# Attention scores of four heads at once in float32, in place of split operands stacked by DMA

## What is computed

```
def _L2_gnn_ref(X, A, Wp, bp, C):          # 8 heads, 32 features each
    Xp = jnp.einsum('bnd,hdk->bhnk', X, Wp) + bp[None, :, None, :]
    Xc = jnp.einsum('bhnk,hjk->bhnj', Xp, C)
    attn = jnp.tanh(A[:, None] * jnp.einsum('bhnj,bhmj->bhnm', Xc, Xp))
    Xh = jnp.einsum('bhnm,bhmk->bhnk', attn, Xp)
    out = jnp.moveaxis(Xh, 1, 2).reshape(X.shape[0], X.shape[1], -1)
    return jax.nn.relu(out)
```

## Time and profile before

| | us |
|---|---|
| median of 3 runs | 1858.39 (1857.15 to 1858.89) |
| span of the profiled execution | 1856.2 |
| PE busy | 1539.5 (83%) |
| DVE busy | 1339.2 (72%) |
| ACT busy | 787.7 (42%) |
| POOL busy | 274.1 (15%) |
| mean granted TensorE clock | 0.924 of full |

### The profile page before, as it was taken

One profiled execution on the slowest core, in us unless ns is written; L12 is line 12 of the kernel. 1 busy time (PEld: TensorE's weight loads), 2 busy tenths in 40 slices (PEclk: granted clock), 3 DMA queues, 4 the chain that ended last, 5 costly groups with the idle time before them and its releaser, 6 DMA issues.

```text
span 1856.2 us, 27152 instructions
## 1 busy us (share of the span) xinstructions
PE 1539.5 (83%) x9334; PEld 1185.5 (64%) x9334; DVE 1339.2 (72%) x3050; ACT 787.7 (42%) x1271; POOL 274.1 (15%) x167
## 2 busy tenths in 40 slices
PE   4587988979798898988989898897989789798855
PEld 3486665757667575766757676675767667576632
DVE  5666868777686877768687776868767686876623
ACT  2224436353453635335353533535353363534432
POOL 1101120111202011120201112020111201012010
PEclk9788999989899898989989898998989899898977
DMA  5013131132313203231320323123031312313030
GB/s 158 12 52 80 52 100 65 38 78 73 90 51 97 67 34 79 73 90 51 86 78 34 79 73 90 51 73 91 23 90 63 101 51 61 83 43 80 22 81 11
DMA packets 80806, 125.52 MB, mean 68 GB/s; under 512 B 10176, under 2 KB 29184, under 8 KB 80768
## 3 DMA queue, kind: packets, MB, share of 16 engines
q1 hardware_dynamic: 80768, 125.02, 24.0%
HBM read 66.27 MB, written 8.39 MB: 40 GB/s over the span
## 4 chain that ended last, share of the span: by engine, by line
PE 56%; DVE 16%; issue 13%; ACT 6%; POOL 5%; SPq 2%; DMA 1%; DVEq 0%; POOLq 0%; ACTq 0%
PE ring_f L1023 32%; PE ring_b L1023 16%; DVE att L969 6%; PE pv_acc L1289 2%; PE ring_f L1179 1%; POOL xp_s L445 1%; POOL xf L428 1%; POOL xf L426 1%; PE ring_f L1209 1%; DVE rows L898 1%; ACT att L596 1%; DVE rows L879 1%; PE ring_f L1121 1%; ACT uz L472 1%; DVE hf L850 1%
## 5 line engine op out<-in xcount | busy, mean ns | idle before, releaser
L1023 PE MATMUL ring_f<-m,inc_n 128*128 128x256 f32 x2048 | 324.2, 288 | 17.0 <-POOL m L418 14.4
L969 DVE TENSOR_TENSOR att<-ring_b,at 128x1024 f32<-128x1024 f32 x256 | 299.2, 1216 | 31.1 <-PE ring_b L1023 30.5
L575 ACT ACTIVATE att<-att 128x1024 f32<-128x1024 f32 x256 | 263.7, 1066 | 100.3 <-DVE att L969 94.4
L1023 PEld LDWEIGHTS ring_f<-m,inc_n 128*128 128x128 f32 x2048 | 289.2, 194 | 25.4 <-issue 21.0
L1023 PE MATMUL ring_b<-stk_c,stk_p 96*128 96x512 f32 x512 | 183.7, 477 | 61.1 <-DMA stk_c<-xc_s 44.5
L1023 PE MATMUL ring_f<-m,inc_t 128*128 128x256 f32 x1024 | 210.3, 284 | 14.5 <-DVE m L728 14.5
L1023 PE MATMUL ring_f<-w,uz 128*128 128x256 f32 (+1 forms) x896 | 188.1, 333 | 13.0 <-DVE uz L721 8.4
L1023 PEld LDWEIGHTS ring_b<-stk_c,stk_p 96*128 96x128 f32 x512 | 97.7, 217 | 147.3 <-issue 70.1
L407 POOL TENSOR_TENSOR rstd_f<-var_f,mhalf 128x4 f32<-128x4 f32 x48 | 48.5, 1010 | 933.2 <-DVE var_f L715 933.2
L1023 PEld LDWEIGHTS ring_f<-w,uz 128*128 128x128 f32 x896 | 151.6, 191 | 34.0 <-DVE uz L721 14.8
L1023 PEld LDWEIGHTS ring_f<-m,inc_t 128*128 128x128 f32 x1024 | 160.4, 191 | 17.7 <-DVE m L728 17.7
(11 more groups left out here) (163 smaller groups left out, 2656.7 us busy)
## 6 DMA issues: line engine op xcount, KB each, us to landing
stk_p<-xp_s SPq DMA_DIRECT2D x192, 128.0 KB, 2.4
stk_c<-xc_s SPq DMA_DIRECT2D x192, 128.0 KB, 2.3
rows<-in_adjT SPq DMA_DIRECT2D x16, 1024.0 KB, 5.3
adj_n<-in_adj SPq DMA_DIRECT2D x16, 1024.0 KB, 8.5
at<-in_adjT SPq DMA_DIRECT2D x16, 1024.0 KB, 5.2
x_in<-in_x SPq DMA_DIRECT2D x16, 512.0 KB, 3.5
out_x<-xb SPq DMA_DIRECT2D x16, 512.0 KB, 2.9
wrow<-in_adj SPq DMA_DIRECT2D x16, 256.0 KB, 6.0
```

Source lines behind the costliest of these rows:

```text
L575: act.activation(v, v, ACT.Tanh).then_inc(tanh_made.sem, 1)
L969: dve.tensor_tensor(att[:, u % 2, 2 * half:2 * half + 2], pair(tile)[:], at[:, t].unsqueeze(1).broadcast_to([P, 2, N]), ALU.mult)\
L1023: ins = pe.matmul(dst, lhsT, rhs, start=(first and n == 0), stop=(last and n == len(pairs) - 1), skip_group_check=True)
```

## The change

The scores are computed in float32 from xp and xc as they are, without split and without stacking. A head's 32 features lie on 32 partitions of its own, so the four heads of a tile use four different groups of 32 array rows, and write four different PSUM banks. Gone are the 24 DMAs of a graph with their two semaphores, the high part of xp on DVE, its low part on POOL and the low part of xc on DVE. ACT writes xp to a buffer of its own (xp_t), and xc with one copy to xc_t. k_scores now waits for both pairs of banks before its first product, where it waited for the second pair after the products of the first. The split of the fourth layer, which used stk_c too, goes to ax_s with unchanged instructions.

```
--- before.py
+++ after.py
@@ buffers and counts @@
-        xp_s = sb("xp_s", [P, 2, 2 * N], F32R)
+        xp_t = sb("xp_t", [P, 2, N])
+        xc_t = sb("xc_t", [P, 2, N])
         xc_s = sb("xc_s", [P, 2, 2 * N], F32R)
-        stk_p = sb("stk_p", [P, HEADS, N], F32R)
-        stk_c = sb("stk_c", [P, HEADS, N], F32R)
+        ax_s = sb("ax_s", [P, 4, N], F32R)
...
@@ SyncE @@
-            def stack(dst, src, part, group, loaded):
-
-                for h in range(4):
-                    sp.dma_start(
-                        dst[32 * group:32 * group + 32, h:HEADS:4, :].bitcast(F32),
-                        src[32 * h:32 * h + 32, part, :].rearrange("p (t n) -> p t n", t=2).bitcast(F32),
-                    ).then_inc(loaded.sem, 16)
-
-            def stack_p(g):
...
-                stack(stk_p, xp_s, 0, 0, stk_p_loaded)
-                stack(stk_p, xp_s, 0, 1, stk_p_loaded)
-                sp.wait_ge(xp_lo_made.sem, xp_lo_made.after(g, 1))
-                stack(stk_p, xp_s, 1, 2, stk_p_loaded)
-
-            def stack_c(g):
...
@@ GpSimd @@
-            def k_xp(g):
-                pool.wait_ge(xp_hi_made.sem, xp_hi_made.after(g, 1))
-                pool.tensor_tensor(xp_s[:, 1], att[:, 0, 0:2].rearrange("p t n -> p (t n)"),
-                                   xp_s[:, 0].bitcast(F32), ALU.subtract).then_inc(xp_lo_made.sem, 1)
@@ ScalarE @@
-                    ins = act.activation(att[:, 0, c], pair(B_XP)[:, c], ACT.Identity, bias=bp_c[:, c:c + 1],
+                    ins = act.activation(xp_t[:, c], pair(B_XP)[:, c], ACT.Identity, bias=bp_c[:, c:c + 1],
                                          scale=1.0)
...
-                act.activation(xc_s[:, 0], pair(B_XC)[:].rearrange("p t n -> p (t n)"), ACT.Copy)\
-                   .then_inc(hi_b_made.sem, 1)
+                act.activation(xc_t[:], pair(B_XC)[:], ACT.Copy).then_inc(copied_b.sem, 1)
@@ VectorE @@
-            def k_xp(g):
...
-                dve.tensor_copy(xp_s[:, 0], att[:, 0, 0:2].rearrange("p t n -> p (t n)")).then_inc(xp_hi_made.sem, 1)
-
-            def k_xc(g):
-                dve.wait_ge(hi_b_made.sem, hi_b_made.after(g, 2))
-                dve.tensor_tensor(xc_s[:, 1], pair(B_XC)[:].rearrange("p t n -> p (t n)"), xc_s[:, 0].bitcast(F32),
-                                  ALU.subtract).then_inc(drained_b.sem, 1)
...
@@ TensorE @@
             def k_scores(g, u):
                 part, t = divmod(u, NT)
                 if u == 0:
-                    pe.wait_ge(stk_p_loaded.sem, stk_p_loaded.after(g, STACK_LOADS))
-                    pe.wait_ge(stk_c_loaded.sem, stk_c_loaded.after(g, STACK_LOADS))
-                for half in range(2):
-                    ps = bank_b(g, B_S + 2 * u + half)
-                    for k in range(2):
-                        h = 4 * part + 2 * half + k
-                        ins = products(ps[:, k], [(stk_p[0:STACK, h, t * P:(t + 1) * P], stk_c[0:STACK, h])])
-                    ins.then_inc(full_b.sem, 1)
+                    pe.wait_ge(copied_b.sem, copied_b.after(g, 2))
+                pairs = [bank_b(g, B_S + 2 * u + half) for half in range(2)]
+                for h in range(4):
+                    rows_of = slice(h * KH, (h + 1) * KH)
+                    ins = pe.matmul(pairs[h // 2][:, h % 2], xp_t[rows_of, part, t * P:(t + 1) * P],
+                                    xc_t[rows_of, part], start=True, stop=True, skip_group_check=True)
+                    if h % 2 == 1:
+                        ins.then_inc(full_b.sem, 1)
```

More of the change, by code:

```diff
@@ L191, in back_drained_at @@
         def back_drained_at(tile):
-            return {B_HT: 1, B_XC: 2, B_OT: 19, B_TT: 20}.get(tile, tile - B_S + 3)
-        STACK_LOADS = 3 * 4
-        STACK = 3 * KH
+            return {B_HT: 1, B_OT: 18, B_TT: 19}.get(tile, tile - B_S + 2)
         x_loaded = Signal(sem("x_loaded"), 1, 16)
@@ L589, in k_ax @@
                 act.wait_ge(full_b.sem, full_b.after(g, B_TT + 1))
-                act.activation(stk_c[:, 0:2], pair(B_TT)[:], ACT.Copy).then_inc(hi_b_made.sem, 1)
+                act.activation(ax_s[:, 0:2], pair(B_TT)[:], ACT.Copy).then_inc(hi_b_made.sem, 1)
             def k_out(g):
@@ L959, in k_unit @@
                     dve.wait_ge(at_loaded.sem, at_loaded.after(g, 1))
-                    dve.wait_ge(xp_lo_made.sem, xp_lo_made.after(g, 1))
-                    dve.wait_ge(full_b.sem, full_b.after(g, B_XN + 1))
                 if u == 1 and seen(g, 1):
@@ L995, in k_ax @@
             def k_ax(g):
-                dve.wait_ge(hi_b_made.sem, hi_b_made.after(g, 3))
-                dve.tensor_tensor(stk_c[:, 2:4], pair(B_TT)[:], stk_c[:, 0:2].bitcast(F32), ALU.subtract)\
+                dve.wait_ge(hi_b_made.sem, hi_b_made.after(g, 2))
+                dve.tensor_tensor(ax_s[:, 2:4], pair(B_TT)[:], ax_s[:, 0:2].bitcast(F32), ALU.subtract)\
                    .then_inc(drained_b.sem, 1)
@@ L1061, in bank_b @@
                                B_O: (B_OT, 0)}.get(tile, (tile - 2, 0))
-                if before in (B_XP, B_XN, B_O):
+                copied = {B_XP: 1, B_XC: 2, B_XN: 3, B_O: 4}
+                if before in copied:
                     if seen(g, ago):
-                        pe.wait_ge(copied_b.sem, copied_b.after(g, {B_XP: 1, B_XN: 2, B_O: 3}[before], ago=ago))
+                        pe.wait_ge(copied_b.sem, copied_b.after(g, copied[before], ago=ago))
                 else:
@@ L1267, in k_xc @@
                 for t in range(2):
-                    ins = products(ps[:, t], [(ct[:, t], att[:, 0, t])])
+                    ins = products(ps[:, t], [(ct[:, t], xp_t[:, t])])
                 ins.then_inc(full_b.sem, 1)
@@ L1281, in k_attend @@
                 if u == 0:
-                    pe.wait_ge(copied_b.sem, copied_b.after(g, 2))
+                    pe.wait_ge(copied_b.sem, copied_b.after(g, 3))
                     if seen(g, 1):
@@ L1327, in k_out @@
                         v = slice(i * P, (i + 1) * P)
-                        pairs += three(stk_c[:, c, v], stk_c[:, 2 + c, v], k3[:, 0, c], k3[:, 1, c])
+                        pairs += three(ax_s[:, c, v], ax_s[:, 2 + c, v], k3[:, 0, c], k3[:, 1, c])
                     ins = products(ps[:, i // 2, (i % 2) * D:(i % 2 + 1) * D], pairs)
```

34 lines of the change are left out of this document (8 added, 26 removed).

## The result

| | before | after |
|---|---|---|
| median of the runs, us | 1858.64 (1857.15 to 1859.56) | 1879.86 (1875.58 to 1880.77) |
| span of the profiled execution, us | 1856.2 | 1878.1 |
| mean granted TensorE clock | 0.924 | 0.94 |

The ratio is 1.0109, with a 95% interval of 1.0097 to 1.0121: the change makes the kernel slower by 21 us. Less work is left to do, and yet it takes longer: the DMAs moved 125.5 MB before and move 75.2 MB now, VectorE's busy time fell from 1339.2 to 1314.4 us and PE's from 1539.5 to 1520.5. PE's mean clock is higher, so it waits more.

A forecast was written before the change was run, and what follows sets the result against it. PE, busy 83% of the span, sets a turn by its order of work. Gross +2.2 less 1.3 from the clock, +0.9 times 15 turns (+13.5), and -7 in the last part gave 1865 us; range 1850 to 1890.

The forecast's parts named there:

- rival (C): Full turns: the clock gives nothing back or returns late; 2.2 us a turn, 1884, up to 1900 us; chance 0.14.
- The DMA wait is covered: PE's 2.46 us wait before k_scores 0 is covered by the 2.56 us ReLU wait before f_hT; gain taken as 0.
- (B): Rival: the DMA wait before k_scores 0 was on the path; -2.46 us a turn, 1815 us; chance 0.04.
- The removed vector work is worth nothing: Removed DVE and POOL parts of xp and xc stand in gaps; removing DVE's 1.22 us only lengthens its wait; gain 0.
- A unit's release at 1.22 us: Score units: DVE may begin 1.22 us after a unit's start, as all four heads finish together; bounds 1.14 to 3.4 plus release.
- The walk through the turn, gross +2.2: From f_hT to k_outT, later releases and the wait for both pairs add 2.2 us a turn; bounds 1.8 to 3.3.
- The clock gives back 1.3: Shifted work lets PE's clock return earlier in the program, saving 1.3 us a turn; net +0.9.
- The bound of 1.85: Most the clock could give back in a full turn: 1.14 + 0.7 = 1.85 us.
- The last back part, -7: Last back part, no front work: 14 us gained on the DMA wait, 7 lost on units and lower clock; -7.
- The sum: Whole kernel: 1856.2 + 13.5 - 7 = 1862.7 us span; runs lie 2.2 above it, 1865 us; chance 0.46.
- (D): Rival: score units' row groups do not run at once; 1985 us, or about 2125 fully in turn; chance 0.12.

The follow-up runs named there:

- e3: Kernel before without its 24 stacking DMAs a graph, score products reading 96 rows of the split operands where they lie: 1845.27 us, 0.9923 of before.
- e7: Kernel after, each pair of banks waited for just ahead of its two heads, with 22 and 9 unused products filling PE's gaps: 1843.08 us, 0.9910 of before.
- e10: Kernel before with 10, 12, 9 and 5 unused products filling PE's gaps: 1832.85 us, 0.9857 of before.
- e9: Kernel after with pair-by-pair waits, 22 and 9 unused products, and one small 128-row product between a unit's second and third product: 1889.63 us, 1.0172 of before.
- e5: Kernel after with 22 unused products ahead of f_hT and 9 between k_out and k_xp: 1863.28 us, 1.0016 of before.
- e8: Kernel after with all four heads of a unit reading array rows 0 to 31, one row group: 2368.3 us, 1.2735 of before.
- e4: Kernel after with 22 unused products between k_scores 0 and f_hT only: 1864.63 us, 1.0030 of before.
- e1: Kernel after with each pair of banks waited for just ahead of its own two products, as in the kernel before: 1860.1 us, 1.0004 of before.

## Why the prediction was right or wrong

The time lies in the range, 15 us above the forecast, and that is in part luck: the forecast was a slowdown of 7 us and 21 were measured, three times as much. The range held it because it was wide enough to take in most of rival (C), at 1884, to which the result is nearest. The place of the loss and its gross size were right; what the clock gives back was not.

- **The DMA wait is covered: right.** f_hT stands 11.00 us behind f_y's start as before, and e3 shows full turns that do not change when the DMAs go. (B) is out.
- **The removed vector work is worth nothing: right.** DVE was 25 us less busy, and k_xp to f_hT, where its removed work stood, is as long in e7 as in e10 (31.26 and 31.25).
- **A unit's release at 1.22 us: measured 1.17**, between the bounds. Its cause was wrong, as e9 shows.
- **The walk through the turn, gross +2.2: right,** 2.15 in a late turn and 33.1 / 15 = 2.2 over the run, between e5 and e10. The parts hold too: the forecast let DVE be idle some 1.2 us before units 6 and 7 (measured 1.23 and 1.23) and had ACT late last before k_outT (1.11 us of idle time on PE, ended by xh_t's copy, where it was 0.81). Unit 2 was to be late by 0.60; against k_attend 0, which was 0.90 us earlier after f_hT, DVE's start moved by 0.40.
- **The clock gives back 1.3: this step failed.** It measured 0.4 a turn in the late turns and 0.24 over the run. The step was built on one early turn that was 1.14 us shorter, and on the thought that a longer program keeps drifting past the good place, and stops there. It did stop, but in a pattern of two turns, of which one keeps the stretch to 5.8 us past f_hT. And the 1.14 was read wrongly. The forecast took it as what the stretch behind f_hT gives back, but that turn has 31.05 us (251.68 to 282.73, rows below) from k_xp to f_hT, where a late turn has 31.86, for the clock was at its upper level behind k_xp (1.00 from 251 to 256 us). Only 0.42 us lie behind f_hT (39.83 us to k_outT and not 40.25). The bound of 1.85 was set too high: behind f_hT the clock costs a late turn of before 1.1 us in all, and 1.66 in the whole turn, so 1.3 was more than there was to give behind f_hT. To take it was to expect the whole cost to vanish, with PE idle for longer ahead of f_hT (5.84 us against 2.46 and 2.56).
- **The last back part, -7: measured -8.0** from the last copy of xc_s. The gain was 13.9 for a forecast 14; the units lost 7.4 for a forecast 4.9 plus 2 for the clock; the 1.3 us won behind the units were in no term. The cycle is 3.74 us (1837.20 to 1840.94) and not 3.53, since DVE idles 1.38 and not 1.26.
- **The sum.** 15 turns by 0.9 were 15 by 1.97 (2.2 - 0.24), 29.5 us for 13.5: that is 16 us too few, less 1 for the last part: the 15 by which the time lies above the forecast.
- **(D): refuted** by 1.07 us a unit, and priced by e8. Its upper end, 2125, does not follow from its own terms: 17 a turn by 15, less 7, is 2106.

The two rows of the early turn, k_xp and f_hT, in the kernel before:

```profile
251.68 2.98 PE L1023 MATMUL ring_b<-xc_s,wp 128*128 128x512 f32 x12 [2.67 <-ACT att L596]
...
282.73 1.97 PE L1179 MATMUL ring_f<-ident,hf 128*128 128x128 f32 x8 [2.06 <-ACT hf L485]
```

## What to carry to other kernels

A transfer that looks like the largest wait can be worth nothing in the steady state and nearly all its length in the last, uncovered part; ask at each wait what is late next. When two engines hand buffers to and fro without a spare one, the time from start to release of each hand-over is the cost, not the busy time: here 0.5 us more a release, with the wait for both pairs (0.54 us of it), made 2 us a turn, though PE, DVE and the DMAs had less to do. And before counting on a shifting clock to pay for a loss, measure what the clock costs at all: filling PE's gaps with products that nobody reads showed it, and gained more (26 us) than all that the DMAs had cost (14 us).

## What the hardware showed that had not been expected

- Two float32 products in different row groups take as long as four: 1.06 against 1.07 us for 512 columns.
- TensorE's granted clock falls around PE's gaps in the full turns here, and a stretch at the lower level outlives the gap (6.0 us past f_hT's start before): products in four places of each turn, in gaps of 1.6 to 2.6 us, raised the mean clock from 0.924 to 0.978 and cut 1.4% off the kernel before.
- A busy PE does not keep its clock up by itself. In e9's last part PE was busy 40.25 of 40.80 us, with score products on 32 rows, 32x32 products and k_attend, at the lower level throughout; e8 had PE busy 91% of the span at a mean of 0.815.
- The same kernel can settle in a pattern over several turns (110.43 and 111.44 us after the change; 110.3 and 111.6 in late turns of e4's profiled execution; 109.9, 110.0 and 111.2 in e1). That a stretch at the lower clock shifts its turn, and so the next stretch, would explain it; no run tests that. A single turn says then little about the others.
